# A decoder layer with a mixture of experts: turned rows rounded from SBUF, row list a step sooner, gathers four tiles ahead, two low halves moved

## The reference, cut to what matters

```python
shared = jnp.einsum('ti,hi->th', jax.nn.silu(x @ sh_gate_w.T) * (x @ sh_up_w.T), sh_down_w)
logits = x @ router_weight.T
probs = jax.nn.softmax(logits.astype(jnp.float32), axis=-1)
top_v, top_i = jax.lax.top_k(probs, TOP_K)
top_v = top_v / top_v.sum(axis=-1, keepdims=True)
combine = (jax.nn.one_hot(top_i, E, dtype=top_v.dtype) * top_v[..., None]).sum(axis=1)
out = jnp.zeros_like(x)
for e in range(E):
    gu = x @ gate_up_proj[e].T
    gate, up = (gu[:, :I_MOE], gu[:, I_MOE:])
    cur = jax.nn.silu(gate) * up @ down_proj[e].T
    out = out + cur * combine[:, e:e + 1]
out = out + jax.nn.sigmoid(x @ shared_gate_w.T) * shared
```

## Time and profile before

| | |
|---|---|
| runs before: median (lowest to highest, 3 runs) | 1735.71 us (1735.0 to 1735.88) |
| the profiled execution: its own time | 1721.43 us |
| its span (first to last instruction) | 1719.6 us |
| busy in the span: PE, PEld, DVE, ACT, POOL | 1685.2, 1519.4, 1219.8, 936.3, 659.3 us |
| instructions | 28891 |

### The profile page before, as it was taken

How to read it: one execution, slowest core, us unless ns; L and a number is a source line. 1 busy time by engine, 2 the same in 40 slices (tenths; PEclk the granted TensorE clock), 3 DMA queues, 4 the chain that set the end, 5 groups by cost and what they waited for, 6 DMA issues and landing times.

```text
span 1719.6 us, 28891 instructions
## 1 busy us (share of the span) xinstructions
PE 1685.2 (98%) x10034; PEld 1519.4 (88%) x10034; DVE 1219.8 (71%) x3379; ACT 936.3 (54%) x1717; POOL 659.3 (38%) x415
## 2 busy tenths in 40 slices
PE   7999999999999999999999999999999999998996
PEld 7998889898989898989898989989898989888986
DVE  5654676878786878777778777776878787746557
ACT  4444455656565656565656565565656565644542
POOL 1210344525243333333334343443525341344525
PEclk9999999999999999999999999999999999999998
DMA  5234643324141423323232323232324130531423
GB/s 197 77 132 134 193 94 78 70 70 80 53 97 41 90 44 87 47 88 67 63 68 63 68 63 68 69 66 77 73 62 90 51 57 12 111 114 35 133 80 98
DMA packets 102856, 140.29 MB, mean 82 GB/s; under 512 B 37022, under 2 KB 81728, under 8 KB 102592
## 3 DMA queue, kind: packets, MB, share of 16 engines
q1 hardware_dynamic: 60784, 115.47, 26.9%
q10 hardware_dynamic: 38912, 14.80, 3.9%
q0 software_dynamic: 3024, 8.26, 1.8%
HBM read 113.62 MB, written 24.89 MB: 81 GB/s over the span
## 4 chain that ended last, share of the span: by engine, by line
PE 91%; DVE 4%; DMA 2%; ACT 1%; POOL 1%; issue 1%; POOLq 0%; SPq 0%; ACTq 0%; DVEq 0%
PE b_turn L831 17%; PE b_out L850 9%; PE b_out L851 9%; PE b_out L852 9%; PE b_score L817 9%; PE b_score L819 9%; PE b_score L818 9%; PE b_out L860 5%; PE a_bank L344 5%; PE c_gate L1511 2%; PE a_bank L370 1%; PE c_down L1538 1%; PE a_bank L395 1%; PE a_bank L424 1%; PE a_bank L417 1%
## 5 line engine op out<-in xcount | busy, mean ns | idle before, releaser
L895 ACT CAST b_pT_hi<-b_turn 125x512 fp32r<-125x512 f32 (+1 forms) x768 | 406.7, 530 | 543.1 <-PE b_turn L831 536.6
L997 DVE TENSOR_TENSOR b_pT_lo<-b_turn,b_pT_hi 125x512 fp32r<-125x512 f32 (+1 forms) x768 | 478.2, 623 | 260.7 <-ACT b_pT_hi L895 254.7
L983 DVE CUSTOM_DVE_ANT_0 b_p<-b_score,b_mask_add 128x500 f32<-128x500 f32 x672 | 452.4, 673 | 58.3 <-PE b_turn L831 24.2
L831 PEld LDWEIGHTS b_turn<-ident,b_p 128*125 128x125 f32 x2688 | 409.8, 187 | 54.8
L831 PE MATMUL b_turn<-ident,b_p 128*125 128x128 f32 x2688 | 418.3, 272 | 0.0
L901 ACT ACTIVATE b_p<-b_p,b_shift 128x1500 f32<-128x1500 f32 x224 | 347.6, 1552 | 2.3 <-DVE b_top_min L991 2.3
L850 PE MATMUL b_out<-b_pT_hi,b_c_hi 125*128 125x512 f32 (+1 forms) x768 | 346.9, 452 | 0.5 <-DVE b_pT_lo L997 0.5
L1135 POOL TENSOR_TENSOR b_oT_lo<-b_oT,b_oT_hi 128x896 fp32r<-128x896 f32 x32 | 67.6, 2114 | 625.6 <-ACT b_oT_hi L925 589.0
L851 PE MATMUL b_out<-b_pT_lo,b_c_hi 125*128 125x512 f32 (+1 forms) x768 | 281.2, 366 | 0.0
L852 PE MATMUL b_out<-b_pT_hi,b_c_lo 125*128 125x512 f32 (+1 forms) x768 | 280.9, 366 | 0.0
L817 PE MATMUL b_score<-b_cT_hi,b_q_hi 128*128 128x500 f32 x672 | 263.2, 392 | 0.0
(11 more groups left out here) (250 smaller groups left out, 2399.8 us busy)
## 6 DMA issues: line engine op xcount, KB each, us to landing
cT_in<-in_ctxT SPq DMA_DIRECT2D x32, 750.0 KB, 10.0
b_c_in<-in_ctx SPq DMA_DIRECT2D x32, 750.0 KB
q_store<-a_fold_in_or_q_stage SPq DMA_DIRECT2D x16, 896.0 KB, 4.1
q_in<-q_store SPq DMA_DIRECT2D x32, 448.0 KB, 4.0
b_rden_all<-rden_store ACTq DMA_DIRECT2D x32, 256.0 KB, 3.6
b_rden_all<-rden_store ACTq DMA_DIRECT2D x32, 192.0 KB, 3.9
b_mask_in<-in_mask SPq DMA_DIRECT2D x32, 187.5 KB, 9.6
slot_store<-c_y2T SPq DMA_DIRECT2D x35, 128.0 KB, 1.7
```

Of the source, the lines that this page charges most:

```text
L831: mm = pe.transpose(turn_bank[n % 3][0:CK, u * 128:(u + 1) * 128], p[slot % 2][:, u, c * CK:(c + 1) * CK], ident[:])
L895: act.copy(pT_hi[:, n % 3, 0:w], turn_bank[n % 3][0:CK, 0:w]).then_inc(hi_done, 1)
L983: dve.tensor_tensor_reduce(out=p[slot % 2][:, u, keys], in0=score_bank[j][:, 0:FW], in1=mask_add[:, b, keys], scale=1.0, scalar=-3.0e38, o ...
L997: dve.tensor_tensor(pT_lo[:, n % 3, 0:w], turn_bank[n % 3][0:CK, 0:w], pT_hi[:, n % 3, 0:w].bitcast(F32), ALU.subtract).then_inc(lo_done, 1)
```

## The change

Four things are changed in `phase_c`.

1. ScalarE rounds a turned half from its own SBUF copy, waiting for that copy, and VectorE subtracts from the copy too; a turn of y2 waits for the copy (`y2T_done`) alone. The copy of a batch waits for the low half of the same columns of the batch before.
2. `at_tile`'s two products go from VectorE to GpSimd (`tokens_of_tiles`), behind the experts that it splits alone. The two `at_place` patterns are made in steps 7 and 8 instead of 8 and 9. `invert` stands ahead of TensorE's step 11 (`INVERT_AT`) and waits for both; `sources` stands ahead of VectorE's step 11.
3. A gather from the fifth on waits for the turn of the tile four before (`X_AHEAD`); the eight places stay.
4. VectorE's two experts' low halves come at the end of its steps 9 and 11 (`RESTS_AT`), and the evacuation of batch 1 behind the first gathered tile.

```diff
--- before.py
+++ after.py
@@ -1249,7 +1249,7 @@
         at_tile = places_2.take("c_at_tile", [128, 2, NT, RP], F32R)
         passed = y2T[:].rearrange("p a n -> p (a n)")[:, 0:2 * NT * RP].rearrange("p (j t n) -> p j t n", j=2, t=NT)
 
-        X_DEEP, Y_DEEP = 8, 4
+        X_DEEP, X_AHEAD, Y_DEEP = 8, 4, 4
         x_in = tiles_0.take("c_x_in", [128, X_DEEP, F])
         xT_hi = tiles_0.take("c_xT_hi", [128, 2, KC, T], F32R)
         xT_lo = tiles_1.take("c_xT_lo", [128, 2, KC, T], F32R)
@@ -1270,7 +1270,7 @@
         e_hi_done, e_ready = sem("e_hi_done"), sem("e_ready")
         y2_turned, y2T_done, y2T_hi_done, y2T_lo_done = sem("y2_turned"), sem("y2T_done"), sem("y2T_hi_done"), sem("y2T_lo_done")
         route_done, route_chain, ex_done, ranked = sem("route_done"), sem("route_chain"), sem("ex_done"), sem("ranked")
-        inverted = sem("inverted")
+        inverted, at_tile_done = sem("inverted"), sem("at_tile_done")
         gate_done, up_done, silu_done, gu_done = sem("gate_done"), sem("up_done"), sem("silu_done"), sem("gu_done")
         h_hi_done, h_lo_done, down_done, z_done = sem("h_hi_done"), sem("h_lo_done"), sem("down_done"), sem("z_done")
         x_loaded = [sem(f"x_loaded{k}") for k in range(X_DEEP)]
@@ -1288,7 +1288,7 @@
         CONSTS, TABLES, SETS = 1, 1, 4
         START_SETS = 2
         COPIED, PICKED, ODDS, COUNTED, GATED = 1, 12, 14, 20, 24
-        PLACED, MATCHED, TABLE_DONE, SOURCED = 33, 41, 44, 45
+        PLACED, PASSED, MATCHED, TABLE_DONE, SOURCED = 33, 37, 39, 42, 43
 
         WHOLE, VECTOR_RESTS, EARLY = 3, 2, 2
         TAIL = attention.tail
@@ -1299,11 +1299,12 @@
         GROUPS = SHARED[:-1]
         FINISH_AT = (0, 0, 0, 0, 0, 0, 2, 2, 2, 1, 0, 0)
         RSTD_AFTER = (7, 10, NT - 1)
-        RESTS_BEHIND = (3, 5, 7)
+        RESTS_BEHIND, RESTS_AT = (3, 5, 7), (9, 11)
         BY_VECTOR = range(SC + WHOLE, SC + WHOLE + VECTOR_RESTS)
         PIECES = SC + EXPERTS
         STEPS = SC * len(SHARED)
         GA = SC * AHEAD
+        INVERT_AT = GA - 1
         HELD_COL = NT * EXPERTS
         SOURCE_COL = 256
         ORDER = [n for first, count in SHARED for n in range(first, first + count)]
@@ -1399,7 +1400,7 @@
                 if kc == 0:
                     pe.wait_ge(y2_loaded[b], 16)
                 if b or kc:
-                    pe.wait_ge(y2T_lo_done, KC * b + kc)
+                    pe.wait_ge(y2T_done, KC * b + kc)
                 else:
                     pe.wait_ge(*attention.fill_taken)
                 for t, n in enumerate(tiles(b)):
@@ -1431,6 +1432,7 @@
 
             def invert():
 
+                pe.wait_ge(at_tile_done, 2)
                 pe.wait_ge(route_chain, MATCHED)
                 for n in range(2 * NT):
                     j, t = n // NT, n % NT
@@ -1486,7 +1488,7 @@
 
                 pe.wait_ge(x_loaded[s % X_DEEP], 16 * (s // X_DEEP + 1))
                 if s < 2:
-                    pe.wait_ge(y2T_lo_done, KC * len(SHARED))
+                    pe.wait_ge(y2T_done, KC * len(SHARED))
                 else:
                     pe.wait_ge(xT_lo_done, s - 1)
                 for kc in range(KC):
@@ -1549,6 +1551,8 @@
                 turning = TURN_AT.index(g) if g in TURN_AT else None
                 if turning == 3:
                     turn_y2(3, 0)
+                if g == INVERT_AT:
+                    invert()
                 hidden(g, 0)
                 if g < 3:
                     route(g)
@@ -1565,7 +1569,6 @@
                     count_places()
                 if g >= LAG:
                     down(g - LAG)
-            invert()
             for g in range(GA - LAG, GA):
                 down(g)
             turn_x(0)
@@ -1598,9 +1601,11 @@
                 w = SHARED[b][1] * T
                 if b:
                     act.wait_ge(route_done, b)
+                    act.wait_ge(y2T_lo_done, KC * (b - 1) + kc + 1)
                 act.wait_ge(y2_turned, KC * b + kc + 1)
                 act.copy(y2T[:, kc, 0:w], turn_bank[:, 0:w]).then_inc(y2T_done, 1)
-                act.copy(y2T_hi[:, kc, cols_of(b)], turn_bank[:, 0:w]).then_inc(y2T_hi_done, 1)
+                act.wait_ge(y2T_done, KC * b + kc + 1)
+                act.copy(y2T_hi[:, kc, cols_of(b)], y2T[:, kc, 0:w]).then_inc(y2T_hi_done, 1)
 
             def round_expert(p):
                 if p == SC + WHOLE:
@@ -1716,7 +1721,7 @@
             def y2T_rest(b, kc):
                 w = SHARED[b][1] * T
                 dve.wait_ge(y2T_hi_done, KC * b + kc + 1)
-                dve.tensor_tensor(y2T_lo[:, kc, cols_of(b)], turn_bank[:, 0:w], y2T_hi[:, kc, cols_of(b)].bitcast(F32),
+                dve.tensor_tensor(y2T_lo[:, kc, cols_of(b)], y2T[:, kc, 0:w], y2T_hi[:, kc, cols_of(b)].bitcast(F32),
                                   ALU.subtract).then_inc(y2T_lo_done, 1)
 
             def copy_logits():
@@ -1780,8 +1785,7 @@
                 seen = passed.rearrange("p j t n -> p (j t) n")
                 link(dve.tensor_tensor(seen, flat(tile_f[:]).unsqueeze(2).to_broadcast([128, 2 * NT, RP]),
                                        tile_number.unsqueeze(1).to_broadcast([128, 2 * NT, RP]), ALU.is_equal))
-                for j in range(2):
-                    link(dve.tensor_tensor(at_tile[:, j], passed[:, j], token.unsqueeze(2).to_broadcast([128, NT, RP]), ALU.mult))
+                assert done == PASSED
 
             def match_places(j):
 
@@ -1907,6 +1911,8 @@
                 if g in TURN_AT:
                     for kc in range(KC):
                         y2T_rest(TURN_AT.index(g), kc)
+                if g == INVERT_AT:
+                    sources()
                 gated(g)
                 if g == 4:
                     copy_logits()
@@ -1929,20 +1935,20 @@
                 if g == 7:
                     split_slots()
                     match_tiles()
-                if g in (8, 9):
-                    match_places(g - 8)
+                if g in (7, 8):
+                    match_places(g - 7)
                 if g == 10:
                     tile_table()
-            sources()
-            for p in BY_VECTOR:
-                expert_rest(p)
-            evacuate(AHEAD - 1)
+                if g in RESTS_AT:
+                    expert_rest(BY_VECTOR[RESTS_AT.index(g)])
             x_rest(0)
             for s in range(RT + 1):
                 if s + 1 < RT:
                     x_rest(s + 1)
                 if s < RT:
                     h_tile(s)
+                if s == 0:
+                    evacuate(AHEAD - 1)
                 if s >= 1:
                     hT_rest(s - 1)
 
@@ -2000,11 +2006,18 @@
                 pool.tensor_tensor(lo, src, hi.bitcast(F32), ALU.subtract)
                 pool.tensor_tensor(lo_down, src_down, hi_down.bitcast(F32), ALU.subtract).then_inc(e_ready, 1)
 
+            def tokens_of_tiles():
+
+                pool.wait_ge(route_chain, PASSED)
+                for j in range(2):
+                    pool.tensor_tensor(at_tile[:, j], passed[:, j], token.unsqueeze(2).to_broadcast([128, NT, RP]),
+                                       ALU.mult).then_inc(at_tile_done, 1)
+
             def fetch_x(s):
                 if s == 0:
                     pool.wait_ge(route_chain, SOURCED)
-                if s >= X_DEEP:
-                    pool.wait_ge(x_turned, s - X_DEEP + 1)
+                if s >= X_AHEAD:
+                    pool.wait_ge(x_turned, s - X_AHEAD + 1)
                 pool.indirect_dma_start(out=x_in[:, s % X_DEEP, :], out_offset=None, in_=D["y2"],
                                         in_offset=bass.IndirectOffsetOnAxis(ap=source[:, s:s + 1], axis=0)).then_inc(
                                             x_loaded[s % X_DEEP], 16)
@@ -2042,6 +2055,7 @@
             rstd_attention()
             for p in range(SC, SC + WHOLE):
                 split(p)
+            tokens_of_tiles()
             for s in range(X_DEEP):
                 fetch_x(s)
                 if s in RESTS_BEHIND:
```

## The result

After: 1726.68 us (median of 6 runs, 1725.75 to 1727.49); before, beside it, 1736.2 (1735.0 to 1737.29). The ratio is 0.9946, 95% interval 0.9936 to 0.9957: 9.5 us less, where 3.45 were forecast. The profiled execution of after took 1727.16 (span 1725.3), like its other runs.

What follows compares the result with a forecast made beforehand. The bound was taken to be the ninth gathered tile, reached by TensorE before it landed. Terms 1.5 + 0.2 + 1.75 (row list 0.8, gathers 0.95) = 3.45 us less, 1735.71 to 1732.2; range 1730.6 to 1734.3.

Steps and rivals of the forecast that it cites:

- Turned rows: Turns of y2: TensorE waits for ScalarE's copy, not VectorE's low half; 1.5 us less for batches 1 and 2, 0.2 for batch 3.
- Row list: VectorE's work up to the list the gathers need: net 1.61 us sooner, less 0.8 of blocking by GpSimd, so 0.8.
- the lock: At the second at_place: VectorE, with two SBUF inputs, waits 0.8 us while GpSimd's at_tile products block it; bounds 0 and 2.5.
- rival (1): at_tile and at_place run side by side, or the block is short: 0.8 us more, 4.25 in all, 1731.5; chance 0.22.
- Gathers: First two expert gathers, 1.70 and 1.44 us beside VectorE's low halves, should near 0.944 with fewer low halves there: 0.95 less.
- rival (2): First two gathers were slow for another reason than VectorE: 0.95 not won, 2.5 us in all, 1733.2; chance 0.13.
- What the ninth tile gains, the kernel gains: Experts: TensorE waits at the ninth gathered tile and for no later gather, so only time won there counts.
- Four ahead: Expert gathers waiting for the turn four tiles before: nothing lands late, so an effect of 0.
- rival 4: Look-ahead too short: gathers land late and TensorE waits at every tile from the ninth on, 1747.9 us; chance 0.04.
- I take the same us off both: Sum made on the profiled execution, 1721.43 us, and subtracted equally from the runs' median, 1735.71, which is 14.3 above.
- The clock term: TensorE's clock at the start of the experts should stay up as its two long gaps shrink; no change by the ninth tile.

Runs made afterwards that it cites:

- experiment 3: The kernel before with only the turned-row change (turns wait for the copy; rounding and difference read it): 1735.68 us, ratio 0.9992.
- experiment 1: The kernel before, unedited, run and traced a second time: 1737.18 us, ratio 1.0002; profiled execution 1735.84.
- experiment 7: The kernel after with VectorE's two experts' low halves back behind the row list, ahead of the first tile: 1726.39 us, ratio 0.9941.
- experiment 5: The kernel after with the last stage's gathers two tiles ahead instead of four: 1723.03 us; three: 1720.61; two, then three: 1722.11. Before with two: 1733.48.
- experiment 6: The kernel after with the experts' gathers two tiles ahead instead of four: 1730.16 us, ratio 0.9965; three ahead: 1724.31, ratio 0.9925.

## Why the prediction was wrong

**Turned rows, 1.5 and 0.2: right.** From the first batch's logits to the second turn of batch 2 it is 8.62 after, 10.38 in the shown trace of before and 10.25 in its second: 1.76 and 1.63, about its upper bound of 1.7; alone, in experiment 3, 1.52. The logits of batch 3 follow 2.85 sooner, of which 0.67 is load wait (0.89 to 0.22).

**Row list, 0.8: too small by what I charged for the lock.** From the product ahead of at_tile and at_place to the list it was 14.48 (1555.17 to 1569.65, experiment 1) and is 12.89 after (1554.60 to 1567.49): 1.59, the unblocked sum of 1.61. The order was as I said, VectorE first: at_tile's row on GpSimd begins at 1555.88 and runs 3.87, to 1559.75, over the whole first at_place, and the Trainium skill's rule (SBUF — State Buffer, Who interferes with whom), that the second of two such instructions is blocked, agrees. But behind that block, ended at 1557.86, both products took 1.9 together instead of 2 times 1.28, and all but 0.2 of it fitted into the 1.68 before the second at_place, which took 2.09 instead of 2.02. The mis-sized term is the price of GpSimd's product, and rival (1) had the right time for the list.

**Gathers, 0.95: nothing won.** The first four took 5.04 before and 5.06 after: instead of 1.70 and 1.44 for the first two, 1.20 for the first and 1.96 for the third, beside the one low half left there. From list to ninth gather it is 20.20 in both shown traces. What rival (2) said of this term (not won) came true, and its reason for a part: the first gather took 1.20 in all ten traces with the changed order, with no low half beside it, so 0.25 is the first gather's own. For the rest VectorE *is* what slows them (3.02 beside two low halves in experiment 7), and not by 0.3: in all ten traces the slow gather ends 0.81 to 0.83 behind the low halves, so it is held until they are done, whenever it started. In four of the ten (experiment 5 with two ahead, both of experiment 6, three ahead in both stages) it is the second gather, 2.15 or 2.16, and TensorE waits 2.0 or 2.1 for the second tile: so that after turned its first two tiles without a wait hung on where a gather met that low half. By the same section of the Trainium skill, which calls it inferred, a tensor_tensor should not hold a gather's descriptors up. The gathers are held up here all the same; whether at their descriptors or where they read their row numbers from SBUF, no run shows.

**What the ninth tile gains, the kernel gains: only half right.** It is turned with no gap after, and with none in experiment 1 either. Its 2.2 are in the result. That the sum up to this tile came near (3.45 forecast, 3.03 measured from the first logits) is luck in part: a list forecast 0.8 too small and a term of 0.95 that was not won cancel. But the thesis came from a trace that lacked what came right behind that tile.

**Four ahead, 0: this is the step that failed.** I asked only whether a gather could come too late (rival 4), not what the gathers do to other engines when nothing holds them back. Eight ahead allowed nine in a row behind the third low half, four ahead allows four or five, and that is worth 6.2 to 7.4 in the runs, 6.2 and 6.5 in the traces, all of it between the ninth tile and the last stage, where ScalarE's slow stretch lies. The parts measured apart, 1.15, 1.6 and 6.2, make 9.0 of the 9.5; the first two are not clear of noise.

**"I take the same us off both": the sign that I passed over.** A profiled execution 14.3 below its runs is not a noisy copy of them: it was an execution without two stretches that the others pay for. The clock term held: 1.00 from 1578 to 1580 after, where the earlier trace rows has 0.50.

What stays open: why a run of gathers slows one engine's issue to steps of 0.7, why ScalarE in the experts and TensorE in the last stage, why four gathers or so are enough in the one place (with eight more ahead of them, among GpSimd's low halves) and eleven are needed in the other, why the one always begins in or behind a block of c_down, and why the shown execution of before was spared both, though its gathers ran without a pause as well (1663.20 to 1681.95 in the last stage).

## What to carry to other kernels

When the profiled execution is well below the timed runs, trace again before pricing anything: the bound may be in what that execution lacks. A look-ahead is not free because nothing is late; a gather that may be issued long before its use will be, in a row with others, and here short pauses between gathers (three tiles ahead instead of eight and four) were worth more than every wait removed from the chain: 1719.24 against 1726.68 and 1736.2. A blocked instruction costs only what does not fit into the blocker's next gap.

## What the runs showed of the hardware that was not expected

Behind eleven or twelve indirect gathers issued 1.25 apart, TensorE's instructions came in steps of 0.7 until the gathers paused, and without gaps some 3 later (the sixteenth gather of after started at 1680.24, the gaps were over by 1684.2), in ten of the eleven traces with such a run; the shown trace of before is the eleventh. TensorE's granted clock fell within the stretch to the lower level (0.51 from 1678 to 1680) and was back at 1688 to 1690 (0.93), so that the stretch is paid for twice. A gather on GpSimd took 1.96 beside one VectorE low half with two inputs in SBUF and 3.02 beside two, instead of 0.95, and ended 0.81 to 0.83 behind the last of them.
